# Moving the eight block transposes of each attention visit from the attention-times-values loop of the visit before into the scores loop of the visit itself

## The chip, the cores and the metric

The kernel runs on the 8 cores of one Trainium2 chip. Every core runs the same program on its own rows of the sequence. The metric is the device time in microseconds of the slowest core. Traces show one core: here core 7, the slowest of the profiled execution.

## What is computed

The reference is one transformer layer over a sequence of 16384 rows of 4096 numbers: a layer norm, an attention with four heads of width 1024 whose queries, keys and values are the normed input times a sign vector, a sigmoid in place of a softmax, a causal mask, a residual, and then a layer norm and a feed-forward step with a low-rank addition.

```python
xh = layernorm(x).reshape(B, T, 4, 1024)
Q, K, V = xh * q_bind, xh * k_bind, xh * v_bind
scores = einsum('bthd,bshd->bhts', Q, K) * 1024 ** -0.5
attn   = where(causal, sigmoid(scores * 4.0), 0.0)
x = x + einsum('bhts,bshd->bthd', attn, V)
x = x + ffn(layernorm(x))        # x @ W.T + bias, and a rank-16 term
```

## The kernel before

**Tiles.** The sequence is cut into 16 blocks of 1024 rows. Core c owns the query blocks c and 15 - c (q = 0 and 1). The attention goes through 8 *sweeps*, one for each query block and head (q outer, h inner). A sweep with q = 0 goes over 8 key blocks k, one with q = 1 over 16, so there are 4 x 8 + 4 x 16 = 96 *visits* (q, h, k). I number them 0 to 95. Sweeps begin at visits 0, 8, 16, 24, 32, 48, 64 and 80. After the attention comes the feed-forward part, which the change doesn't touch.

**One visit** is made by these pieces of the program, which write instructions into one list for each engine. Every engine runs its own list in order.

- `plan_visit_prep` (line 473): eight 512 KB loads on SyncE's queue bring the raw key block, one subtile of 128 rows each, into two buffers `khd`. VectorE normalises each subtile into `xb` (line 488). A load into a `khd` buffer waits until VectorE has normalised what was in it, so only two loads can run ahead of VectorE. Then one 1 MB load of the mask `msk` is issued, which waits until the masks of the visit before were used. It returns eight *tasks*; each task is `plan_xpose` (line 372) for one subtile: eight 128x128 transposes on TensorE into a PSUM buffer `ptr` (line 383, two buffers) and one copy by VectorE into `xbT` (line 394).
- `plan_qk_sig` (line 505): for each of eight key subtiles `sc`, TensorE waits for the copy into `xbT` of that subtile, and makes two groups of eight matmuls (line 517) into one of four PSUM banks. ScalarE takes the sigmoid of each group (line 531), VectorE multiplies it by the mask into `attn` (line 539). If statistics tasks are left, one follows each group: a 1 MB load on GpSimd's queue into one of two buffers `kh`, a VectorE sum (line 331) and two ScalarE sums of squares (lines 335, 338). Every 17th task is a short chain of small VectorE operations and a square root (lines 350 to 371). There are 272 tasks; they fill the first 16 visits and nine groups of visit 16.
- `plan_av` (line 552): 16 groups of eight matmuls (line 563) into two PSUM banks `pav`; VectorE adds each group into `acc` (line 580).
- `plan_epilogue` (line 594), after the last visit of a sweep: two small matmuls (line 597), their copies (line 602), and for each of eight subtiles two VectorE operations (lines 615, 617) and a store from one buffer `ebuf`.
- `plan_qg_prep`, ahead of each sweep: eight loads, each followed by a VectorE normalisation (line 417), eight transposes (line 430) and eight VectorE multiplies (line 441).

**The order before** is written out by the loop at line 671. For visit i the lists get: scores of visit i; then, if i + 1 starts a sweep, `plan_qg_prep`; then the eight normalisations of visit i + 1; then attention-times-values of visit i, in which after every second group one transpose task of visit i + 1 follows; then the epilogue, if visit i ends a sweep. So on VectorE the eight normalisations of the next visit stand ahead of the sixteen adds into `acc` of this one.

Of the kernel before, what the change touches and what calls it, by code (L numbers as in the profile page):

```python
# [25 lines left out]
def build_program():  # L26
# [24 lines left out]
    def ap_(e, fn):  # L51
        plan[e].append(fn)

    def W(e, sem, v):
        if v <= 0 or hiw[e][sem] >= v:
            return
        hiw[e][sem] = v
        ap_(e, lambda E, s=sem, vv=v: E.wait_ge(SEM[s], vv))
# [7 lines left out]
    def op(e, sem, build, n=1):  # L66
        if e in SERIAL:
            W(e, SERIAL[e], cnt[SERIAL[e]])
        v = bump(sem, n)
        ap_(e, lambda E, b=build, s=sem, k=n: b(E).then_inc(SEM[s], k))  # L70
        return v

    def opq(e, build):
        if e in SERIAL:
            op(e, SERIAL[e], build)
            return
        ap_(e, lambda E, b=build: b(E))
# [20 lines left out]
    with contextlib.ExitStack() as SH:  # L98
# [176 lines left out]
        with contextlib.ExitStack() as AT:  # L275
# [226 lines left out]
                         for st in range(NS)]  # L502
                return evs, mdv, tasks

            def plan_qk_sig(q, h, k, evs, mdv):
                b = k % 2
                gi = 0
                ttv = 0
                for sc in range(NS):
                    W("t", "V", evs[sc])  # L510
                    for th in range(2):
                        bank = gi % 4
                        qk_bank[bank].acquire("t")
                        qv = None
                        for dc in range(NS):
                            bf_ = (lambda E, dc=dc, sc=sc, th=th, b=b, bank=bank:
                                   E.matmul(  # L517
                                       pqk[bank][:],
                                       xbT[b][:, HD * dc + 128 * sc:HD * dc + 128 * (sc + 1)],
                                       QgT[:, CH * dc + 512 * th:CH * dc + 512 * (th + 1)],  # L520
                                       start=(dc == 0), stop=(dc == NS - 1)))
                            if dc == NS - 1:
                                qv = op("t", "T", bf_)
                            else:
                                opq("t", bf_)
                        state["qk_last"] = qv
                        ss = gi % 2
                        stage_slot[ss].acquire("s")
                        W("s", "T", qv)
                        W("s", "G", g_const)  # L530
                        sgv = op("s", "S", lambda E, ss=ss, bank=bank: E.activation(  # L531
                            out=stage[ss][:], in_=pqk[bank][:], func=AF.Sigmoid,
                            scale=cst[:, 0:1]))
                        qk_bank[bank].release([("S", sgv)])
                        W("v", "S", sgv)
                        W("v", *mdv)
                        W("v", "T", state["attn_war"])
                        ttv = op("v", "V", lambda E, ss=ss, sc=sc, th=th:
                                 E.tensor_tensor(  # L539
                                     attn[:, CH * sc + 512 * th:CH * sc + 512 * (th + 1)],  # L540
                                     stage[ss][:],
                                     msk[:, CH * sc + 512 * th:CH * sc + 512 * (th + 1)],
                                     OP.mult))
                        stage_slot[ss].release([("V", ttv)])
                        gi += 1
                        if stat_tasks:
                            stat_tasks.popleft()()
                            stat_drained[0] += 1
                msk_slot.release([("V", ttv)])
                return ttv  # L550

            def plan_av(q, h, k, ttv, xtasks):
                b = k % 2
                W("t", "V", ttv)
                gj = 0
                for tc in range(NS):
                    for dh in range(2):
                        bank = gj % 2
                        av_bank[bank].acquire("t")
                        avv = None  # L560
                        for sc in range(NS):
                            bf_ = (lambda E, sc=sc, tc=tc, dh=dh, b=b, bank=bank:
                                   E.matmul(  # L563
                                       pav[bank][:],
                                       attn[:, CH * sc + 128 * tc:CH * sc + 128 * (tc + 1)],
                                       xb[b][:, HD * sc + 512 * dh:HD * sc + 512 * (dh + 1)],
                                       start=(sc == 0), stop=(sc == NS - 1)))
                            if sc == NS - 1:
                                avv = op("t", "T", bf_)
                            else:  # L570
                                opq("t", bf_)
                        state["av_last"] = avv
                        W("v", "T", avv)
                        dst = acc[:, CH * tc + 512 * dh:CH * tc + 512 * (dh + 1)]
                        if k == 0:
                            sv = op("v", "V", lambda E, d=dst, bank=bank:
                                    E.tensor_copy(d, pav[bank][:]))
                        else:
                            sv = op("v", "V", lambda E, d=dst, bank=bank:
                                    E.scalar_tensor_tensor(  # L580
                                        out=d, in0=pav[bank][:], scalar=1.0, in1=d,
                                        op0=OP.mult, op1=OP.add))
                        av_bank[bank].release([("V", sv)])
                        gj += 1
                        if gj % 2 == 0 and xtasks:
                            xtasks.pop(0)()
                while xtasks:
                    xtasks.pop(0)()
                xb_slot[b].release([("T", state["av_last"])])
                xbT_slot[b].release([("T", state["qk_last"])])  # L590
                state["attn_war"] = state["av_last"]
# [69 lines left out]
            def drain_stats_until(kind, idx):  # L661
                tgt = stat_group_end.get((kind, idx), 0)
                while stat_drained[0] < tgt and stat_tasks:
                    stat_tasks.popleft()()
                    stat_drained[0] += 1

            plan_qg_prep(0, sweeps[0][0], sweeps[0][1])
            evs0, mdv0, tasks0 = plan_visit_prep(sweeps[0][0], sweeps[0][1], 0)
            for t_ in tasks0:
                t_()  # L670
            prepped = {0: (evs0, mdv0)}

            for fi, (sidx, q, h, k, L) in enumerate(flat):
                evs, mdv = prepped.pop(fi)
                ttv = plan_qk_sig(q, h, k, evs, mdv)
                ntasks = []
                if fi + 1 < len(flat):
                    nsidx, nq, nh, nk, nL = flat[fi + 1]
                    if nk == 0:
                        if nh == 0:  # L680
                            drain_stats_until("q", nq)
                        plan_qg_prep(nsidx, nq, nh)
                    if nh == 0:
                        drain_stats_until("kv", nk)
                    nevs, nmdv, ntasks = plan_visit_prep(nq, nh, nk)
                    prepped[fi + 1] = (nevs, nmdv)
                plan_av(q, h, k, ttv, ntasks)
                if k == L - 1:
                    plan_epilogue(sidx, q, h)

            fin = dict(cnt)

# [271 lines left out]
```

How the kernel before makes its waits and increments, by code:

```python
    def W(e, sem, v):  # L54
        if v <= 0 or hiw[e][sem] >= v:
            return
        hiw[e][sem] = v
        ap_(e, lambda E, s=sem, vv=v: E.wait_ge(SEM[s], vv))
# [7 lines left out]
    def op(e, sem, build, n=1):  # L66
        if e in SERIAL:
            W(e, SERIAL[e], cnt[SERIAL[e]])
        v = bump(sem, n)
        ap_(e, lambda E, b=build, s=sem, k=n: b(E).then_inc(SEM[s], k))
        return v
```

## Time and profile before

| | us |
|---|---|
| median of 3 runs | 12455.98 |
| the 3 runs | 12455.98, 12600.02, 12022.85 |
| profiled execution, whole | 11592.07 |
| profiled execution, span of core 7 | 11590.5 |
| spans of the 8 cores in it | 11547.0 to 11590.5 |

The profiled execution is shorter than each of the three runs. All sums in this document are made against it, since all durations come from it.

On the page, times are in microseconds unless marked ns. PE is TensorE's matmuls, PEld its weight loads, DVE is VectorE, ACT ScalarE, POOL GpSimd, SP SyncE. L563 is line 563 of the kernel before. In a timeline each row is: start, duration, engine, line, operation, output<-inputs, shapes, count, and in brackets the idle time just before and what ended it. Rows with the same operation in a run are merged. In a table of windows the columns are: the window, its length, the busy time and the number of instructions of PE, PEld, DVE, ACT and POOL, TensorE's granted clock as a share of the full one, the busy share of the DMA engines, and GB/s.

### The profile page before, as it was taken

How to read it: one execution, taken by the hardware profiler on the slowest of the kernel's cores; microseconds unless marked ns; L12 is line 12 of the kernel's file. 1: busy time of each engine (PE TensorE's matmuls, PEld its weight loads, DVE VectorE, ACT ScalarE, POOL GpSimd, SP SyncE). 2: the span in 40 equal slices, each digit the busy share in tenths (PEclk: the TensorE clock that was granted, in tenths of full speed). 3: DMA queues.
4: the chain of work that ended last, by engine and by line, in shares of the span. 5: the costliest groups of instructions: out<-in, count | busy, mean ns of one | idle time of the engine just before them, and what ended most of it. 6: DMA issues, size and time to landing. Idle time of an engine off the chain costs nothing.

```text
span 11590.5 us, 107337 instructions; the slowest of 8 cores (11547.0 to 11590.5 us)
## 1 busy us (share of the span) xinstructions
PE 7240.2 (62%) x36337; PEld 3343.7 (29%) x36337; DVE 4714.1 (41%) x6433; ACT 1864.7 (16%) x2891; POOL 260.1 (2%) x494
## 2 busy tenths in 40 slices
PE   0055545554775766777567775777757777378488
PEld 0022212221332332333233332333323333123233
DVE  2455555554444444444444444444444444410300
ACT  0234423331111111111011110111101111100100
POOL 0000000000000000000000000000000000000000
PEclk9987767777887888888888887888878888689699
DMA  9555544454222222121322122212131212144233
GB/s 110 153 170 175 174 132 166 167 174 129 75 69 73 73 69 77 55 73 55 80 66 73 55 73 73 73 55 73 55 91 55 73 55 73 44 105 98 67 80 91
DMA packets 503829, 1065.63 MB, mean 92 GB/s; under 512 B 315829, under 2 KB 315845, under 8 KB 451013
## 3 DMA queue, kind: packets, MB, share of 16 engines
q1 hardware_dynamic: 445336, 672.85, 20.1%
q0 software_dynamic: 57952, 385.92, 11.2%
q8 instruction: 298, 4.88, 0.2%
q14 instruction: 243, 1.99, 0.1%
HBM read 974.72 MB, written 83.89 MB: 91 GB/s over the span
## 4 chain that ended last, share of the span: by engine, by line
PE 53%; DMA 24%; DVE 11%; issue 5%; ACT 3%; SPq 2%; another core or an unknown queue 1%; DVEq 1%; ACTq 0%; POOLq 0%; POOL 0%
PE pav L563 22%; PE pqk L517 19%; DMA khd<-xk 14%; PE py L863 8%; DMA kh<-xk 5%; DVE xb L488 3%; PE ptr L383 3%; SPq L84 2%; DMA x1s<-ebuf 2%; DVE QgT L441 1%; ACT sdump L335 1%; ACT stage L531 1%; DVE suc L331 1%; DMA kh<-xq 1%
## 5 line engine op out<-in xcount | busy, mean ns | idle before, releaser
L563 PE MATMUL pav<-xb,attn 128*128 128x512 bf16 x12288 | 3016.3, 402 | 2189.0 <-DVE acc L580 1675.5
L517 PE MATMUL pqk<-QgT,xbT 128*128 128x512 bf16 x12288 | 2828.4, 392 | 699.8 <-ACT stage L531 687.7
L563 PEld LDWEIGHTS pav<-xb,attn 128*128 128x128 bf16 x12288 | 1222.4, 102 | 3700.7 <-issue 2567.7
L531 ACT ACTIVATE stage<-pqk,cst 128x512 bf16<-128x512 f32 x1536 | 1055.7, 687 | 6703.2 <-PE pqk L517 5825.9
L517 PEld LDWEIGHTS pqk<-QgT,xbT 128*128 128x128 bf16 x12288 | 1215.3, 100 | 2270.8 <-issue 944.6
L539 DVE TENSOR_TENSOR attn<-stage,msk 128x512 bf16<-128x512 bf16 x1536 | 1063.6, 692 | 1527.9 <-ACT stage L531 1523.4
L580 DVE SCALAR_TENSOR_TENSOR acc<-pav,acc 128x512 f32<-128x512 f32 x1408 | 974.1, 692 | 1262.8 <-PE pav L563 1217.5
L488 DVE TENSOR_SCALAR xb<-khd,mcache,rcache 128x1024 bf16<-128x1024 f32 x768 | 624.0, 813 | 1491.1 <-DMA khd<-xk 1469.7
L863 PE MATMUL py<-wtb,h2T 128*128 128x512 bf16 x4096 | 917.1, 382 | 221.0 <-DMA wtb<-wb 221.0
L331 DVE TENSOR_REDUCE suc<-kh 128x1 f32<-128x2048 f32 x288 | 658.3, 2286 | 264.6 <-DMA kh<-xk 196.7
L863 PEld LDWEIGHTS py<-wtb,h2T 128*128 128x128 bf16 x4096 | 392.9, 98 | 737.3 <-issue 290.6
L394 DVE COPY xbT<-ptr 128x1024 bf16<-128x1024 bf16 x768 | 531.4, 692 | 81.7 <-DVE acc L580 1.8
L884 DVE SCALAR_TENSOR_TENSOR yb<-py,xsl 128x512 f32<-128x512 f32 x128 | 88.6, 692 | 1109.4 <-PE py L873 1109.4
L383 PE MATMUL ptr<-ident,xb 128*128 128x128 bf16 x6144 | 471.7, 220 | 46.2 <-DVE xb L488 28.1
L383 PEld LDWEIGHTS ptr<-ident,xb 128*128 128x128 bf16 x6144 | 409.4, 98 | 229.0 <-issue 52.3
L335 ACT ACTIVATE sdump<-kh 128x1024 bf16<-128x1024 f32 x288 | 304.3, 1056 | 719.0 <-DMA kh<-xk 375.6
L430 PE MATMUL ptr<-ident,qtm 128*128 128x128 bf16 x512 | 63.5, 302 | 451.6 <-DVE qtm L417 451.6
L338 ACT ACTIVATE sdump<-kh 128x1024 bf16<-128x1024 f32 x288 | 304.3, 1056 | 26.9 <-ACT sdump L335 0.7
L787 PE MATMUL ptrF<-ident,fb 128*128 128x128 bf16 x512 | 64.8, 306 | 373.0 <-DVE fb L776 373.0
L746 ACT ACTIVATE sdump<-fb 128x1024 bf16<-128x1024 bf16 x64 | 67.6, 1056 | 889.1 <-DMA fb<-x1s 884.7
L615 DVE TENSOR_TENSOR ebuf<-acc,vbsl 128x1024 bf16<-128x1024 f32 x64 | 78.4, 1225 | 301.7 <-DMA x1s<-ebuf 300.9
L441 DVE TENSOR_SCALAR QgT<-ptr,gT 128x128 bf16<-128x128 bf16 x512 | 145.4, 284 | 135.1 <-PE ptr L430 85.4
(110 smaller groups left out, 1292.5 us busy)
## 6 DMA issues: line engine op xcount, KB each, us to landing
khd<-xk SPq DMA_DIRECT2D x768, 512.0 KB, 5.0
kh<-xk POOLq DMA_DIRECT2D x256, 1024.0 KB, 5.5
msk<-mk SPq DMA_DIRECT2D x96, 1024.0 KB, 8.6
khd<-xq SPq DMA_DIRECT2D x128, 512.0 KB, 4.3
wb<-wgt POOLq DMA_DIRECT2D x4, 8192.0 KB, 202.0
kh<-xq POOLq DMA_DIRECT2D x32, 1024.0 KB, 6.1
y<-yb POOLq DMA_DIRECT2D x128, 256.0 KB, 2.3
x1s<-ebuf POOLq DMA_DIRECT2D x64, 256.0 KB, 4.5
```

The source lines that it names most:

```text
L331: opq("v", lambda E, col=col: E.reduce_sum(suc[:, col:col + 1], kr_ap, axis=AX))
L335: opq("s", lambda E, col=col: E.activation(out=sdump[:], in_=kr_ap[:, 0:1024], func=AF.Square, accum_out=sqa[:, 2 * col:2 * col + 1]))
L338: sv = op("s", "S", lambda E, col=col: E.activation(out=sdump[:], in_=kr_ap[:, 1024:2048], func=AF.Square, accum_out=sqa[:, 2 * col + 1:2 ...
L383: bf_ = (lambda E, dc=dc, xo=xb_buf, c0=st * HD, p=ps: E.transpose(ptr[p][:, 128 * dc:128 * (dc + 1)], xo[:, c0 + 128 * dc:c0 + 128 * (dc ...
L394: ev = op("v", "V", lambda E, d=dst, s_=src: E.tensor_copy(d, s_))
L488: E.tensor_scalar(out=xb[b][:, st * HD:(st + 1) * HD], in0=khd[ks][:], scalar1=mcache[:, 8 * k + st:8 * k + st + 1], scalar2=rcache[:, 8 * ...
L517: E.matmul(pqk[bank][:], xbT[b][:, HD * dc + 128 * sc:HD * dc + 128 * (sc + 1)], QgT[:, CH * dc + 512 * th:CH * dc + 512 * (th + 1)], star ...
L531: sgv = op("s", "S", lambda E, ss=ss, bank=bank: E.activation(out=stage[ss][:], in_=pqk[bank][:], func=AF.Sigmoid, scale=cst[:, 0:1]))
L539: E.tensor_tensor(attn[:, CH * sc + 512 * th:CH * sc + 512 * (th + 1)], stage[ss][:], msk[:, CH * sc + 512 * th:CH * sc + 512 * (th + 1)], ...
L563: E.matmul(pav[bank][:], attn[:, CH * sc + 128 * tc:CH * sc + 128 * (tc + 1)], xb[b][:, HD * sc + 512 * dh:HD * sc + 512 * (dh + 1)], star ...
L580: E.scalar_tensor_tensor(out=d, in0=pav[bank][:], scalar=1.0, in1=d, op0=OP.mult, op1=OP.add))
L863: E.matmul(py[bank][:], h2T[:, 1024 * dc + 128 * tc:1024 * dc + 128 * (tc + 1)], wtt[:, 512 * dc:512 * (dc + 1)], start=(dc == 0), stop=Fa ...
```

## The change

It reorders the program's lists; no operation is added or taken away. The transpose tasks of a visit go from `plan_av` of the visit before to `plan_qk_sig` of the visit itself: one ahead of each subtile `sc`. And all preparation of visit i + 1 (query preparation, rest of the statistics, loads and normalisations) now follows `plan_av` and the epilogue of visit i, where it stood ahead of them.

```diff
-            def plan_qk_sig(q, h, k, evs, mdv):
+            def plan_qk_sig(q, h, k, evs, mdv, xtasks):
...
                 for sc in range(NS):
+                    if xtasks:
+                        xtasks.pop(0)()
                     W("t", "V", evs[sc])
...
-            def plan_av(q, h, k, ttv, xtasks):
+            def plan_av(q, h, k, ttv):
...
-                        if gj % 2 == 0 and xtasks:
-                            xtasks.pop(0)()
-                while xtasks:
-                    xtasks.pop(0)()
...
-            prepped = {0: (evs0, mdv0)}
+            prepped = {0: (evs0, mdv0, [])}
...
-                evs, mdv = prepped.pop(fi)
-                ttv = plan_qk_sig(q, h, k, evs, mdv)
-                ntasks = []
+                evs, mdv, xtasks = prepped.pop(fi)
+                ttv = plan_qk_sig(q, h, k, evs, mdv, xtasks)
+                plan_av(q, h, k, ttv)
+                if k == L - 1:
+                    plan_epilogue(sidx, q, h)
                 if fi + 1 < len(flat):
...
                     nevs, nmdv, ntasks = plan_visit_prep(nq, nh, nk)
-                    prepped[fi + 1] = (nevs, nmdv)
-                plan_av(q, h, k, ttv, ntasks)
-                if k == L - 1:
-                    plan_epilogue(sidx, q, h)
+                    prepped[fi + 1] = (nevs, nmdv, ntasks)
```

## Rows read from the trace of the kernel before

**Rows 1.** The page: busy time by engine, share of the span, instructions.

```profile
PE 7240.2 (62%) x36337; PEld 3343.7 (29%) x36337; DVE 4714.1 (41%) x6433; ACT 1864.7 (16%) x2891; POOL 260.1 (2%) x494
```

**Rows 2.** The waits: engine, tile and line, waiting for; us in total, times, longest.

```profile
PE pav L563 <- DVE acc L580: 1675.5, 87, 25.0
```

**Rows 3.** Timeline of an ordinary visit inside a sweep, TensorE and VectorE.

```profile
6063.02 27.79 PE L517 MATMUL pqk<-QgT,xbT 128*128 128x512 bf16 x128
...
6092.62 1.74 DVE L488 TENSOR_SCALAR xb<-khd,mcache,rcache 128x1024 bf16<-128x1024 f32 x2
...
6092.66 3.61 PE L563 MATMUL pav<-xb,attn 128*128 128x512 bf16 x16 [1.85 <-DVE attn L539]
...
6113.34 0.81 DVE L488 TENSOR_SCALAR xb<-khd,mcache,rcache 128x1024 bf16<-128x1024 f32 x1 [3.98 <-DMA khd<-xk]
...
6115.09 5.96 PE L563 MATMUL pav<-xb,attn 128*128 128x512 bf16 x16 [18.37 <-DVE acc L580]
...
6120.89 0.61 PE L383 MATMUL ptr<-ident,xb 128*128 128x128 bf16 x8
...
6121.34 3.62 PE L563 MATMUL pav<-xb,attn 128*128 128x512 bf16 x16
...
6122.03 0.69 DVE L394 COPY xbT<-ptr 128x1024 bf16<-128x1024 bf16 x1
```

**Rows 4.** Windows that hold whole visits, from scores start to scores start.

```profile
734.50:1520.40 785.90, 431.82 (x1925) 181.55 (x1923) 438.35 (x463) 303.24 (x498) 50.67 (x96) 0.77 0.50 169
1520.40:1878.40 358.00, 157.47 (x710) 67.69 (x708) 187.18 (x231) 97.30 (x160) 20.69 (x39) 0.69 0.47 150
1878.40:2650.10 771.70, 431.79 (x1924) 183.12 (x1922) 424.62 (x457) 289.43 (x474) 47.94 (x90) 0.77 0.48 164
2650.10:2987.70 337.60, 149.72 (x709) 66.69 (x707) 171.13 (x236) 80.38 (x130) 15.42 (x29) 0.72 0.40 128
3506.60:3684.50 177.90, 72.07 (x386) 35.76 (x386) 79.83 (x138) 10.99 (x16) 4.34 (x8) 0.68 0.31 89
8711.50:9858.30 1146.80, 856.55 (x4483) 406.65 (x4481) 478.54 (x673) 153.99 (x224) 0.00 (x0) 0.88 0.21 65
```

**Rows 5.** Timeline of visit 95, which has no next visit to prepare.

```profile
9887.96 27.79 PE L563 MATMUL pav<-xb,attn 128*128 128x512 bf16 x128 [1.85 <-DVE attn L539]
...
9915.92 0.69 DVE L580 SCALAR_TENSOR_TENSOR acc<-pav,acc 128x512 f32<-128x512 f32 x1 [1.03 <-PE pav L563]
```

**Rows 6.** Timeline of a sweep's end (visits 23, 24), TensorE and VectorE.

```profile
3508.39 0.81 DVE L417 TENSOR_SCALAR qtm<-khd,omc,orc 128x1024 bf16<-128x1024 f32 x1
...
3551.11 0.81 DVE L488 TENSOR_SCALAR xb<-khd,mcache,rcache 128x1024 bf16<-128x1024 f32 x1
...
3572.57 0.81 DVE L488 TENSOR_SCALAR xb<-khd,mcache,rcache 128x1024 bf16<-128x1024 f32 x1 [4.07 <-DMA khd<-xk]
...
3603.00 0.60 PE L597 MATMUL pqk<-vbrow,ones_b 1*128 1x512 bf16 x2
...
3662.13 1.23 DVE L617 TENSOR_TENSOR ebuf<-ebuf,khd 128x1024 bf16<-128x1024 bf16 x1
```

**Rows 7.** Timeline of visit 6's end, with statistics tasks.

```profile
1441.21 2.29 DVE L331 TENSOR_REDUCE suc<-kh 128x1 f32<-128x2048 f32 x1
...
1460.17 5.54 PE L563 MATMUL pav<-xb,attn 128*128 128x512 bf16 x16 [16.31 <-DVE attn L539]
...
1462.52 0.17 DVE L350 TENSOR_TENSOR ve<-suc 128x8 f32<-128x8 f32 x1
...
1467.95 0.17 DVE L371 TENSOR_TENSOR rcache<-r,t 128x8 f32<-128x8 f32 x1
```

**Rows 8.** Timeline of visit 7's scores: TensorE after rests of different length.

```profile
1537.37 3.57 PE L517 MATMUL pqk<-QgT,xbT 128*128 128x512 bf16 x8 [4.42 <-ACT stage L531]
...
1546.87 6.55 PE L517 MATMUL pqk<-QgT,xbT 128*128 128x512 bf16 x16 [3.01 <-ACT stage L531]
```

**Rows 9.** The mask's load, from issue to landing.

```profile
DMA to landing us min/median/max: 6.6/8.6/9.9
```

## The prediction

> **What bounds the kernel now.** I read the busy shares first. TensorE is the busiest engine with 62% of the span, VectorE has 41% [rows 1]: no engine is full, so the order of work and its waits set the time. The list of waits names the one to look at: the attention-times-values matmuls wait 1675.5 us in 87 places for the adds into `acc` [rows 2]. Then I read the timeline of an ordinary visit, one without statistics tasks and inside a sweep [rows 3]. The scores take 27.79 us without a break, 0.217 us a matmul, so TensorE is at its full clock of 2.4 GHz there. It rests 1.85 us until the last sigmoid and mask multiply are through. It makes two groups of attention-times-values (3.61 us) and stops for 18.37 us: both PSUM banks are full, and VectorE, which must empty them, has the eight normalisations of the next visit ahead of them in its list. These run from 6092.62 to 6113.34 + 0.81 = 6114.15, a stretch of 21.5 us in which VectorE mostly waits for loads, since two buffers let only two loads run ahead. After the stop the first 16 matmuls take 5.96 us where the next 16 take 3.62: 2.3 us for the clock. Then 8 transposes (0.61 us on TensorE) follow every second group, and their copy by VectorE (0.69 us) runs beside the matmuls and holds up nobody. Fourteen such visits take 1146.8 us [rows 4], 81.9 us each.
>
> **Part 1: the stop in attention-times-values goes.** After the change VectorE's list has the 16 adds right behind the mask multiplies. Visit 95 shows what that gives, as it has nothing to prepare: 128 matmuls in 27.79 us [rows 5]. In an ordinary visit before, the same matmuls with the transposes took 81.9 - 27.8 - 1.85 = 52.3 us.
>
> **Part 2: the same stop comes back ahead of the scores.** The normalisations now start after the last add. The scores need the first copy into `xbT`, and that stands behind all eight normalisations on VectorE. From the end of the matmuls: last add through 0.86 us later (9915.92 + 0.69, against 9887.96 + 27.79 [rows 5]), 0.1 to the next instruction, the stretch of normalisations, 0.1 + 0.69 for the copy [rows 3], 0.06 to TensorE. The stretch is 21.5 us in one visit [rows 3] and 22.3 in another [rows 6]; I take 22.0. Nothing in it is sped up: the buffers are still two, and the first two loads were ready before too. So TensorE rests 0.86 + 0.1 + 22.0 + 0.85 = 23.8 us, where it rested about 19. Before, two groups of matmuls lay beside the stretch; now nothing does but the first transposes, 0.61 us. The slow start of the clock, 2.2 us, moves with the stop.
>
> **Part 3: a lockstep inside the scores.** This decides the case. The copy for subtile sc + 1 now stands on VectorE behind both mask multiplies of subtile sc, and TensorE waits for that copy before the next matmul. Its four banks no longer let it run ahead. The row that prices the wait is the 1.85 us between scores and attention-times-values [rows 3]: it is the same chain, last matmul, sigmoid, mask multiply, next matmul. The copy adds 0.69 + 0.06. So each of seven places costs 1.85 + 0.75 = 2.60 us; the transposes fit inside it, since TensorE does them while ScalarE works. That is 18.2 us a visit. Lower bound: the chain can't be shorter than its three durations, about 2.1 us, or 14.7 a visit.
>
> **The ordinary visit after:** scores 27.8 + 2.2 + 18.2 = 48.2; 1.85; attention-times-values 27.8; rest 23.8. Sum 101.6, against 81.9: **+19.7 us**. In parts: the stop +4.5, lockstep +18.2, the transposes leave the other loop -3.1. There are 73 such visits (17 to 94 without the five that end a sweep): +1,440 us.
>
> **The clock in the lockstep.** After the 1.85 us rest the next matmuls run at the full rate, 3.61 us for 16, each time [rows 3]. After rests of 4.42 and 3.01 us they ran at about half rate (3.57 us for 8, 6.55 for 16) [rows 8]. In the lockstep TensorE does 0.61 us of transposes and then rests 2.0 us, so I keep the full rate; the other case is a rival below. The Trainium skill (TensorE: Matmul & The Clock Gate, section "HAM oscillation — how this bites in real kernels") says that short bursts of matmuls between waits can each start at the half clock; by that rule each pair of groups in the lockstep would be slow if the rest were long enough. The rests of 3.01 and 4.42 us agree with it, the one of 1.85 us lies on the other side.
>
> **Sweep ends.** Before, the epilogue on VectorE ran beside only four groups of the next scores, and the query preparation beside nothing. Now everything is in one row. From scores end to scores end: 1.85 + 27.8 + epilogue 60.4 (3603.0 to 3662.13 + 1.23) + query preparation 42.7 (3508.39 to 3551.11) + normalisations 22.3 (to 3572.57 + 0.81) [rows 6] + 0.85 + 48.2 = 204.1, against 177.9 [rows 4]: +26.2, five times: +131.
>
> **Visits with statistics.** Each group there brings a 2.29 us sum on VectorE and 2.5 us on ScalarE. Before, the loads set the pace and TensorE waited 16.31 us at the end of the scores [rows 7]. After, I follow one subtile from the copy: first group at half clock 3.4 (3.57 in [rows 8]), sigmoid 0.9, multiply 0.85, sum 2.4; second multiply 0.7 and sum 2.4, copy 0.75, and some 0.4 in which the second sigmoid waits for the slow second group: 11.8 us. With the clock up it would be 10.0. The scores with their tail are 7 x 11.8 + 8.65 = 91.2. Visits 1 to 6 then take 91.2 + 27.8 + 23.8 + 5.6 for the last statistics task (1462.52 to 1467.95 + 0.17 and a gap [rows 7]), which had stood elsewhere: 148.5 against 785.9 / 6 = 131.0, +105 for six. Visits 9 to 14: 142.8 against 771.7 / 6 = 128.6, +85. Visits 7 and 8: 91.2 + 27.8 + 60.4 + 42.7 + 22.3 + 0.85 = 245.3, and 142.8, against 358.0: +30. Visits 15 and 16 (nine tasks in 16): 245.3 + 125.2 against 337.6: +33 [rows 4]. Visit 0 has no lockstep: -4. Visit 95: +20. Together +269.
>
> **Costs at nothing.** SyncE's queue: the order of loads is the same but for the sweep ends, where the epilogue's loads now precede the preparation's; they have the same two buffers and are paced by VectorE either way. The mask load is issued about 8 us before the normalisations end and takes at most 9.9 us [rows 9]; its first reader now comes some 5 us after their end, so about 3 us are to spare. If that cover went, each microsecond of lateness would be 95 us in all. GpSimd's queue: the stores of the epilogue wait for VectorE as before; behind them stand only statistics loads.
>
> **The sum:** 1,440 + 131 + 269 = +1,840 us. 11,592 + 1,840 = **13,430 us** for an execution like the profiled one. The three runs of before lie 431 to 1,008 us above that execution, and no row says why. The matmuls are the same after, so some of it will be there too; TensorE rests more, so I take the smallest: 13,430 + 430 = **13,860 us**.
>
> The Trainium skill (TensorE: Matmul & The Clock Gate, section "Seeing it yourself") says that dense matmuls on three or more cores of a die are held below the full clock; the profiled execution shows nothing of it, with 0.217 us a matmul.
>
> **The rivals.**
> - *The clock falls in the lockstep.* For it: the rests of 3 us and more [rows 8]. Against: 1.85 us never did. 16 matmuls would take 6.55 instead of 3.47 us: +3.1 in seven places of 79 visits, +1,700. 15,130 us on the profiled basis.
> - *The stretch of normalisations shrinks*, because the loads land faster once attention-times-values no longer runs beside them. Against: only 3.6 us of matmuls ran beside them before, and these don't load anything. Its floor is 8 x 0.81 = 6.5 us, 15.4 less in 79 visits, -1,220: 12,210 us, still slower than 11,592 by 5%.
> - *Not slower: what lengthens the runs outside the profile is spared.* If the 431 to 1,008 us come from dense matmul stretches, and the looser stretches after escape them altogether, after stands at 13,430 and before at up to 12,600. That is +6.6%. To end within 2%, before would have to gain 1,590 us that after does not; the highest run shows 1,008. The place is the 27.8 us stretches of scores, which the lockstep breaks up.
>
> **How the numbers follow.** The forecast has 0.86, the clock 0.08, the shorter stretch 0.04, the spared excess 0.02. The range reaches down to 13,430 less the warm statistics chain (1.8 x 8 x 15 = 216), so 13,200, and up to 13,430 + 1,008 and some 150 for the terms, 14,600. It leaves out the clock rival and the shorter stretch, 0.12 together. About 2% is what a measurement of this kernel can tell from no change; even the floor of the stretch lies outside it. Slower by over 2%: 0.97; within: 0.02; faster: 0.01.
>
> **What the profile after would show.** The wait of the `pav` matmuls for `acc` gone, and their 128 in 27.8 us. In the scores, 16 matmuls, 8 transposes, and then a rest of about 2.0 us ended by the copy into `xbT`, seven times a visit; a first rest of about 23 us. Visits of 101.6 us. VectorE's busy time unchanged at 4,714 us. If the rest in the scores is near 1 us, or the pairs take 6.5 us, part 3 is wrong; if the first rest is far from 23, part 2; if visits with statistics are not longer by 14 to 17 us, their chain.

## The result and the profile after

| | us |
|---|---|
| changed kernel, median of 9 runs | 14428.37 (13901.96 to 14566.09) |
| kernel before, median of 10 runs | 12082.18 (11587.66 to 12639.78) |
| ratio of comparable runs | 1.205, 95% interval 1.190 to 1.220 |
| least disturbed execution, before and after | 11,588 and 13,902: +2,314 |

The forecast was slower, 13,860 us in a range of 13,200 to 14,600; the kernel is slower, at 14,428. Every one of its nine runs is longer than the longest of the kernel before. The runs of one kernel spread here by 2 to 13%, because in some of them the cores of one die or both show a lower granted clock, so what follows compares the runs and cores without it, called undisturbed. The cores of the profiled execution of the changed kernel:

```profile
core 0: 13921.1 us, clock 0.815
core 1: 13908.7 us, clock 0.816
...
core 5: 14332.1 us, clock 0.787
```

I read core 0, whose span is within 0.2% of the 13,902 us. It stands against the 13,430 us of the forecast for an execution like the profiled one of before: the sum was 490 us short, 1,840 where some 2,330 came. Its waits answer to [rows 2]:

```profile
PE pqk L519 <- DVE xbT L394: 3931.1, 760, 23.0
DVE attn L541 <- ACT stage L533: 3718.0, 1518, 6.2
```

The matmuls into `pav`, which waited 1675.5 us for `acc` before [rows 2], wait for it nowhere now. In place of that wait the scores' matmuls wait 3931.1 us for the copy into `xbT`, in 760 places: eight for each of visits 1 to 95. Busy time didn't move: VectorE has 4713.6 us on the page of the changed kernel, 4714.1 before [rows 1]. All the loss is waiting and clock: VectorE makes nothing more than before, but TensorE waits for it in more places.

The timeline of core 0, from the end of one visit through the scores of the next (line 565 is attention-times-values, 519 the scores, 541 the mask multiply, 383 and 394 the transposes and their copy):

```profile
7012.32 0.69 DVE L541 TENSOR_TENSOR attn<-stage,msk 128x512 bf16<-128x512 bf16 x1 [1.05 <-ACT stage L533]
7013.16 27.79 PE L565 MATMUL pav<-xb,attn 128*128 128x512 bf16 x128 [1.85 <-DVE attn L541]
...
7041.92 1.73 DVE L488 TENSOR_SCALAR xb<-khd,mcache,rcache 128x1024 bf16<-128x1024 f32 x2
...
7062.31 0.81 DVE L488 TENSOR_SCALAR xb<-khd,mcache,rcache 128x1024 bf16<-128x1024 f32 x1 [2.23 <-DMA khd<-xk]
7063.23 0.69 DVE L394 COPY xbT<-ptr 128x1024 bf16<-128x1024 bf16 x1
7064.17 5.24 PE L519 MATMUL pqk<-QgT,xbT 128*128 128x512 bf16 x16 [20.68 <-DVE xbT L394]
...
7072.17 3.61 PE L519 MATMUL pqk<-QgT,xbT 128*128 128x512 bf16 x16 [2.31 <-DVE xbT L394]
7074.21 0.69 ACT L533 ACTIVATE stage<-pqk,cst 128x512 bf16<-128x512 f32 x1 [3.95 <-PE pqk L519]
7075.07 0.69 DVE L541 TENSOR_TENSOR attn<-stage,msk 128x512 bf16<-128x512 bf16 x1 [3.15 <-ACT stage L533]
7075.62 0.61 PE L383 MATMUL ptr<-ident,xb 128*128 128x128 bf16 x8
7075.94 0.69 ACT L533 ACTIVATE stage<-pqk,cst 128x512 bf16<-128x512 f32 x1 [1.04 <-PE pqk L519]
7076.79 0.69 DVE L541 TENSOR_TENSOR attn<-stage,msk 128x512 bf16<-128x512 bf16 x1 [1.03 <-ACT stage L533]
7077.59 0.69 DVE L394 COPY xbT<-ptr 128x1024 bf16<-128x1024 bf16 x1
7078.54 3.61 PE L519 MATMUL pqk<-QgT,xbT 128*128 128x512 bf16 x16 [2.31 <-DVE xbT L394]
...
7091.27 5.30 PE L519 MATMUL pqk<-QgT,xbT 128*128 128x512 bf16 x16 [2.31 <-DVE xbT L394]
...
7099.32 3.61 PE L519 MATMUL pqk<-QgT,xbT 128*128 128x512 bf16 x16 [2.31 <-DVE xbT L394]
```

Attention-times-values runs through in 27.79 us, as in [rows 5]. It starts 0.15 us after the end of the last mask multiply (7012.32 + 0.69). The normalisations take 21.2 us (7041.92 to 7062.31 + 0.81), as before, now with TensorE at rest. Then comes the lockstep, to be followed from 7072.17: matmuls, sigmoid at 7075.94, mask multiply at 7076.79, copy at 7077.59, next matmuls at 7078.54. And one pair of groups, at 7091.27, takes 5.30 us instead of 3.61.

The last 14 whole visits of this core, from scores start to scores start (columns as in [rows 4]):

```profile
10674.50:12164.20 1489.70, 913.97 (x4481) 416.19 (x4482) 478.61 (x672) 153.89 (x224) 0.00 (x0) 0.86 0.16 50
```

That is 106.4 us a visit; [rows 4] has 81.9 and the forecast 101.6.

### The profile page after: what moved, and what is told of

Its sections match the earlier page's. It is cut to its first block, busy times and chain, and to the rows that moved or that the text cites. A ratio compares the mean times of both kernels' runs of the same rounds, so it can differ in the third digit from the quotient of the medians.

```text
span 14332.1 us, 107914 instructions; the slowest of 8 cores (13908.7 to 14332.1 us)
## 1 busy us (share of the span) xinstructions
PE 8099.5 (57%) x36337; PEld 3545.8 (25%) x36337; DVE 4713.6 (33%) x6433; ACT 1864.7 (13%) x2891; POOL 259.6 (2%) x494
## 4 chain that ended last, share of the span: by engine, by line
PE 53%; DVE 17%; DMA 15%; issue 6%; ACT 6%; SPq 2%; another core or an unknown queue 1%; DVEq 1%; ACTq 0%; POOLq 0%; POOL 0%
PE pqk L519 24%; PE pav L565 20%; DMA khd<-xk 11%; PE py L860 7%; ACT stage L533 4%; DVE attn L541 4%; DVE xbT L394 4%; DVE xb L488 3%; DVE suc L331 2%; SPq L84 2%; DMA x1s<-ebuf 2%; DVE QgT L441 1%; DVEq L58 1%; ACT sdump L335 1%
## 5 line engine op out<-in xcount | busy, mean ns | idle before, releaser
L519 PE MATMUL pqk<-QgT,xbT 128*128 128x512 bf16 x12288 | 3572.8, 456 | 3966.0 <-DVE xbT L394 3947.4
L565 PE MATMUL pav<-xb,attn 128*128 128x512 bf16 x12288 | 2816.1, 394 | 207.9 <-DVE attn L541 207.9
L519 PEld LDWEIGHTS pqk<-QgT,xbT 128*128 128x128 bf16 x12288 | 1335.4, 113 | 5950.1 <-issue 5257.9
L860 PE MATMUL py<-wtb,h2T 128*128 128x512 bf16 x4096 | 1080.8, 431 | 221.4 <-DMA wtb<-wb 221.4
L860 PEld LDWEIGHTS py<-wtb,h2T 128*128 128x128 bf16 x4096 | 428.7, 107 | 865.1 <-issue 800.9
L430 PEld LDWEIGHTS ptr<-ident,qtm 128*128 128x128 bf16 x512 | 49.5, 138 | 852.7 <-issue 852.7
L84 POOL DMA_DIRECT2D x1s<-ebuf x64 | 34.6, 541 | 9486.2 <-DVE ebuf L615 9486.2
```

The costliest lines, as they stand in the source:

```text
L84: E.dma_start(out=o, in_=i, **kww), 16)
L519: E.matmul(pqk[bank][:], xbT[b][:, HD * dc + 128 * sc:HD * dc + 128 * (sc + 1)], QgT[:, CH * dc + 512 * th:CH * dc + 512 * (th + 1)], star ...
L565: E.matmul(pav[bank][:], attn[:, CH * sc + 128 * tc:CH * sc + 128 * (tc + 1)], xb[b][:, HD * sc + 512 * dh:HD * sc + 512 * (dh + 1)], star ...
L860: E.matmul(py[bank][:], h2T[:, 1024 * dc + 128 * tc:1024 * dc + 128 * (tc + 1)], wtt[:, 512 * dc:512 * (dc + 1)], start=(dc == 0), stop=Fa ...
```

## Experiments

Theory L: the lockstep in the scores is the bulk of the loss. Rival P: the normalisations, now exposed, are. Theory K: what is missing in the sum is TensorE's clock, which falls in the short rests of the lockstep. Two kernels part L from P by undoing one half of the change each; two change the length of the rest, one in each direction; the changed kernel itself runs beside them once more; and one takes the stop out of the kernel before without making a lockstep.

### One half undone: transposes a subtile ahead

```diff
                 for sc in range(NS):
-                    if xtasks:
+                    while xtasks and len(xtasks) > NS - 2 - sc:
                         xtasks.pop(0)()
```

> Changed kernel, but each transpose task is written one subtile earlier: tasks 0 and 1 ahead of the first scores, task sc + 1 ahead of the scores of subtile sc, so the copy into xbT stands on VectorE ahead of the mask multiplies and TensorE needn't wait for them. The preparation stays behind attention-times-values. Theory L (the lockstep is the bulk of the loss): the seven rests in the scores go, 7 x 2.9 us and about 3.0 us of slow clock, and 7 x 0.43 us of transposes come into the open: an ordinary visit of 106.4 becomes 86 us, with the rest of 23.5 us ahead of the scores kept. In all some 1,800 us less than the changed kernel: 12,100 us, 4 to 5% over before. Rival P (the exposed normalisations are the bulk): the visit stays above 100 us and the kernel near 13,900 us.

Measured: 11,903 us undisturbed (11,924 in a second run, 12,307 and 12,901 in the other two) against 11,593 of before beside it. The wait and the timeline of core 2 of this kernel:

```profile
PE pqk L519 <- DVE xbT L394: 2049.7, 144, 21.8
...
7016.73 1.49 DVE L394 COPY xbT<-ptr 128x1024 bf16<-128x1024 bf16 x2
7017.67 5.90 PE L519 MATMUL pqk<-QgT,xbT 128*128 128x512 bf16 x16 [19.33 <-DVE xbT L394]
7023.41 0.61 PE L383 MATMUL ptr<-ident,xb 128*128 128x128 bf16 x8
7023.86 3.62 PE L519 MATMUL pqk<-QgT,xbT 128*128 128x512 bf16 x16
7025.38 0.69 DVE L394 COPY xbT<-ptr 128x1024 bf16<-128x1024 bf16 x1
7027.31 0.61 PE L383 MATMUL ptr<-ident,xb 128*128 128x128 bf16 x8
7027.76 3.62 PE L519 MATMUL pqk<-QgT,xbT 128*128 128x512 bf16 x16
```

and its last 14 whole visits:

```profile
8929.40:10126.50 1197.10, 863.51 (x4480) 406.81 (x4480) 478.52 (x673) 153.89 (x224) 0.00 (x0) 0.86 0.18 62
```

85.5 us a visit, where L wanted 86 and P over 100. The wait for the copy stands in 144 places instead of 760. There is no rest at all between the pairs, and the only slow pair is the first one, behind the long rest. 2,000 of the 2,314 us are gone with one line, 200 more than L said. What stays, 310 us, goes with the new place of the preparation: the rest ahead of the scores is there as in the changed kernel. P falls.

### The other half undone: preparation back in its old place

```diff
                 ttv = plan_qk_sig(q, h, k, evs, mdv, xtasks)
-                plan_av(q, h, k, ttv)
-                if k == L - 1:
-                    plan_epilogue(sidx, q, h)
                 if fi + 1 < len(flat):
...
                     prepped[fi + 1] = (nevs, nmdv, ntasks)
+                plan_av(q, h, k, ttv)
+                if k == L - 1:
+                    plan_epilogue(sidx, q, h)
```

> The other half: preparation of the next visit back ahead of attention-times-values, as in the kernel before, but the transposes one subtile at a time inside the scores, as in the changed kernel. Theory L: an ordinary visit is 81.9 - 3.1 for the transposes + 1.9 for the first copy + 7 x 2.9 + 3.0 for the clock = 104 us, the kernel 13,650 us, 17 to 18% over before. Rival P: about as before, 82 us a visit and 11,600 us.

Measured: 13,850 us undisturbed, the lowest of six runs (up to 14,654), where P wanted 11,600 and L 13,650. The waits of core 4 in the profiled execution, whose span is 14,181 us:

```profile
PE pqk L519 <- DVE xbT L394: 2485.8, 760, 62.3
PE pav L565 <- DVE acc L582: 1675.2, 87, 26.4
```

Both waits are there side by side: the old stop, 1675.2 us where [rows 2] has 1675.5, and a wait for the copy in the same 760 places as in the changed kernel. The lockstep alone costs about as much as the whole change. The two halves cost 310 and 2,260 us, more together than the 2,314 of the whole. Two terms of the expectations are in the halves and not in the whole: the transposes that lie in the open in the first half (7 x 0.43 us a visit), and the 1.9 us for the first copy in this one. That they make up the difference is an argument; no run takes it apart.

### The rest filled with transposes nobody needs

```diff
+                for dc in [d for _r in range(2) for d in range(NS)]:
+                    opq("t", lambda E, dc=dc, xo=xb_buf, c0=st * HD, p=ps:
+                        E.transpose(
+                            ptr[p][:, 128 * dc:128 * (dc + 1)],
+                            xo[:, c0 + 128 * dc:c0 + 128 * (dc + 1)], ident[:]))
                 for dc in range(NS):
```

> Changed kernel with each group of eight transposes in a visit done three times into the same PSUM buffer (the same result, 16 more transposes of 0.056 us each a subtile, about 0.9 us). They lie in the rest of 2.3 us before the copy, whose start the sigmoids and mask multiplies set, so by themselves they cost nothing. Theory K (in a quarter of the subtiles the clock has fallen in the rest, which makes 16 matmuls 5.2 us instead of 3.6): with a rest of 1.4 us no pair starts slow, the visit goes from 106.4 to 103.4 us and the kernel from 13,900 to about 13,650 us, though it does more. If the slow pairs come from something else, they stay, and the time is 13,900 or more.

Measured: 14,033 to 14,620 us in four runs, which alone would not tell it from the changed kernel. But in the shortest of them cores 4 to 7 took 13,635 to 13,681 us, where the same four cores took 13,839 to 13,894 in a run of the changed kernel. That speaks for K, and the profile of a second measurement settles it.

> The kernel with the filled rest once more, beside the changed kernel on the same chip, for a profile that can be compared pair by pair. Theory K: no pair of groups behind a rest of 1.4 us takes 5.0 us or more where the changed kernel has about one in four at 5.2; the visit is 103.4 us and the span 13,650 us. Otherwise the slow pairs stay.

Measured: 13,687 and 13,695 us in two of four runs (14,386 and 14,449 in the others). The timeline of TensorE on core 5 (line 524 is the scores, 384 the added transposes, 388 the needed ones):

```profile
7071.65 3.61 PE L524 MATMUL pqk<-QgT,xbT 128*128 128x512 bf16 x16 [1.41 <-DVE xbT L399]
7075.10 1.06 PE L384 MATMUL ptr<-ident,xb 128*128 128x128 bf16 x16
7076.00 0.61 PE L388 MATMUL ptr<-ident,xb 128*128 128x128 bf16 x8
7078.02 3.61 PE L524 MATMUL pqk<-QgT,xbT 128*128 128x512 bf16 x16 [1.41 <-DVE xbT L399]
...
10482.20:11933.50 1451.30, 976.75 (x6272) 507.78 (x6273) 478.51 (x672) 153.93 (x224) 0.00 (x0) 0.89 0.16 51
```

The pair still starts 6.37 us after the one before (7071.65 to 7078.02), as in the changed kernel (7072.17 to 7078.54): the added work lies wholly in the rest. But of 540 such pairs that the trace shows as one row after the statistics visits, all 540 take 3.61 us; on core 0 of the changed kernel 389 of 526 do, and 137 take 5.0 to 5.3. The visit is 103.7 us instead of 106.4, and the kernel 215 us faster with 12,288 more transposes. K holds. The added work does two things at once, though: it shortens the rest and gives TensorE more to do between two pairs. Which of the two keeps the clock up, this run can't tell.

### The rest made longer: each copy twice

```diff
+                opq("v", lambda E, d=dst, s_=src: E.tensor_copy(d, s_))
                 ev = op("v", "V", lambda E, d=dst, s_=src: E.tensor_copy(d, s_))
```

> Changed kernel with each copy into xbT made twice (the same result). VectorE's busy time grows by 96 x 8 x 0.69 = 530 us. Theory L: the copy is on the path of every subtile, so each of the eight places costs 0.8 us more, 6.4 us a visit, 610 us in all, and the wait of the scores' matmuls for the copy grows by as much. Theory K adds: the rest of TensorE grows from 2.3 to 3.1 us, so more pairs of groups start with the clock down, up to all seven a visit where about one in four does now: up to 8.5 us a visit more. So 14,500 us with L alone, up to 15,300 with K at its most, against 13,900 of the changed kernel. If the copy lay beside other work, nothing would be added.

Measured: 15,378 us, the lowest of four runs (up to 15,729). Rows of core 7 (span 15,243), its wait for the copy, pairs of scores and the window of the last 14 visits:

```profile
PE pqk L520 <- DVE xbT L395: 4551.2, 760, 24.8
...
7005.32 3.61 PE L520 MATMUL pqk<-QgT,xbT 128*128 128x512 bf16 x16 [3.10 <-DVE xbT L395]
...
7029.82 5.30 PE L520 MATMUL pqk<-QgT,xbT 128*128 128x512 bf16 x16 [3.10 <-DVE xbT L395]
...
7038.68 6.49 PE L520 MATMUL pqk<-QgT,xbT 128*128 128x512 bf16 x16 [3.10 <-DVE xbT L395]
...
11763.70:13473.60 1709.90, 1043.97 (x4480) 448.93 (x4481) 556.06 (x784) 154.42 (x224) 0.00 (x0) 0.78 0.14 43
```

The rest grew from 2.31 to 3.10 us, by the 0.79 of a copy and its gap: the copy lies on the path, as L says. The wait for it grew from 3931.1 to 4551.2 us, by 620 where L said 610. Of the 553 pairs behind a short rest in visits 17 to 95 only 104 are at full speed now, 309 take 4.8 to 5.4 us and 140 take 6.3 to 6.6. The starts of the single matmuls in the trace say what these times are: 0.216 us apart at full clock, 0.427 at half. A pair of 6.5 us has 13 or 14 of its 15 intervals at half clock, one of 5.3 us has 8. And not all slow pairs start slow: the one at 7029.82 has four intervals at full clock and only then eight near half. Of the 553 pairs 273 start at half clock and 176 fall to it after three to six intervals. The last 14 visits take 122.1 us each, 15.7 more than in the changed kernel: 6.4 for the copies, some 9 for the clock, where K at its most had said 8.5. Over all 73 ordinary visits it is 121.2 against 106.5, some 8 for the clock.

### The changed kernel beside them

> The changed kernel itself, beside the two others on the same chip, as their measure. Span 13,900 us; TensorE's rests before the copy 2.3 us, about one pair of groups in four at 5.2 us instead of 3.6.

Measured: 14,390 to 14,910 us in six runs. In the profiled one cores 0 to 3 took 13,865 to 13,900 us, where the eight cores of the kernel with the filled rest took 13,639 to 13,693 beside it. Core 1 shows 400 of 534 pairs at 3.6 us and 134 at 5.0 to 5.3: the share of slow pairs is a quarter again.

### A version that beats both: normalisations between the groups

It starts from the kernel before. Each normalisation is a task too, and `plan_av` takes one ahead of every two groups; the mask load follows the last.

```diff
-            def plan_av(q, h, k, ttv, xtasks):
+            def plan_av(q, h, k, ttv, xtasks, ntask):
...
                 for tc in range(NS):
+                    if ntask:
+                        ntask.pop(0)()
                     for dh in range(2):
```

> Kernel before, but the eight normalisations of the next visit are not ahead of attention-times-values: one stands ahead of each two groups of it, the transposes of that subtile after them as before, the mask load after the last. VectorE then has two adds, a normalisation and a copy (2.9 us) to each 3.9 us of TensorE, and the loads get 3.9 us each where they took 2.75. If the stop in attention-times-values comes only from the order on VectorE's list, it goes and doesn't come back: a visit of 27.8 + 1.85 + 27.8 + 8 x 0.43 = 61 us against 81.9, some 1,900 us less than before, 9,700 us. If the loads can't keep that pace beside the matmuls, a rest of a few us stays ahead of every second pair and the visit is 65 to 75 us.

Measured: 9,571 us undisturbed, 10,073 the median of six runs, against 11,593 and 11,940 of before beside it: 17% less undisturbed (the expectation said 9,700 us), and 31% less than the changed kernel's 13,902. Core 5 (line 573 is attention-times-values, 489 the normalisation, 590 the add):

```profile
6049.29 3.62 PE L573 MATMUL pav<-xb,attn 128*128 128x512 bf16 x16
6049.98 0.69 DVE L394 COPY xbT<-ptr 128x1024 bf16<-128x1024 bf16 x1
6050.78 0.81 DVE L489 TENSOR_SCALAR xb<-khd,mcache,rcache 128x1024 bf16<-128x1024 f32 x1
6051.69 0.69 DVE L590 SCALAR_TENSOR_TENSOR acc<-pav,acc 128x512 f32<-128x512 f32 x1
6052.75 0.61 PE L383 MATMUL ptr<-ident,xb 128*128 128x128 bf16 x8
6053.09 0.69 DVE L590 SCALAR_TENSOR_TENSOR acc<-pav,acc 128x512 f32<-128x512 f32 x1 [0.70 <-PE pav L573]
6053.19 3.62 PE L573 MATMUL pav<-xb,attn 128*128 128x512 bf16 x16
...
6959.20:7812.90 853.70, 827.44 (x4483) 400.03 (x4481) 478.15 (x673) 154.18 (x224) 0.00 (x0) 1.00 0.28 87
```

In each 3.90 us of TensorE VectorE does a copy, a normalisation and two adds and still waits 0.70 us for TensorE; no wait for a load is listed for these 14 visits. The visit is 61.0 us, to the tenth what was expected, with a granted clock of 1.00 over the window: the stop took the slow restart with it.

## Why the prediction was right, and where its sum was short

**Slower, by a lockstep: right.** Both halves of the change, each alone, show that part 3 of the prediction is the bulk of the loss: without the lockstep 310 of 2,314 us are left, with the lockstep alone 2,260 come. The stop in attention-times-values goes (part 1) and comes back ahead of the scores (part 2): the time from the end of its matmuls to the scores is 23.5 us on average, forecast 23.8. The stretch of normalisations stayed at 21 to 22 us; the rival by which it shrinks didn't happen. VectorE's busy time didn't change. The mask load was nowhere waited for.

**The price of one place in the lockstep: 2.90 us, not 2.60.** A pair starts 6.37 us after the last where the sum had 3.47 + 2.60. Two small errors add up. The 1.85 us were a rest counted from the modelled end of the last matmul, which lies 3.61 us behind the start of a pair, and I added them to the 3.47 us that a pair takes inside an unbroken run: 0.14 us lost. And I gave the copy 0.69 + 0.06: it starts 0.11 us behind the mask multiply, and TensorE starts 0.26 us behind its end (7077.59 + 0.69 to 7078.54), where it starts 0.15 behind a mask multiply (7013.16). The copy adds 0.11 + 0.69 + 0.26 - 0.15 = 0.91. Seven places make 2.1 us a visit. The term "lockstep +18.2" measured 20.3.

**"So I keep the full rate": the step that failed.** I took the 1.85 us rest, never followed by slow matmuls, as the nearest row to a rest of 2.0, and put the whole clock into a rival in which all pairs would be slow, by 3.1 us each. The 1.85 us rest was no bad reading: in the changed kernel too it is never followed by slow matmuls (0 of 77 visits on core 0). But the rest in the lockstep is 2.3 us, and 137 of 526 pairs are slow by about 1.65 us: 0.26 x 7 x 1.65 = 3.0 us a visit. The forecast was one case, its rival the other, and the chip did a quarter of the rival's pairs at about half of its price for each. The run with the filled rest and the one with the longer rest show that it hangs on what happens between the pairs: none, a quarter, four fifths of the pairs have a slow stretch where the rests are 1.4, 2.3 and 3.1 us. Why a quarter, and not all or none, no run shows.

**The sum, then,** on core 0. Ordinary visits 106.47 on average instead of 101.6: 73 x 4.9 = +355 (2.1 + 3.0 - 0.3 for the rest ahead of the scores). Sweep ends 208.6 instead of 204.1, +23. Visits 0 to 16 together about +105: the chain there took 93.6 us from scores start to attention-times-values in the first sweep (forecast 91.2), and 96.5 in the second, for which I have no experiment. Visits 1 to 6 and 9 to 14 became 22 us longer on average, more than the 14 to 17 that the prediction had set as the sign that their chain was right. The three terms add up to some 485 of the 490.

**From the profiled basis to the median.** I had added 430 us, the least that the three runs of before showed. The median of the changed kernel lies 526 us above its least disturbed run (14,428 - 13,902). In the kernel before it lies 494 us above. With all the 490 us that the sum lacked the forecast would have been 14,350. That the looser stretches are spared what lengthens the runs is not borne out. Some luck is in the range: its top allowed 150 us for errors of the sum, and they came to 490. The median lies inside it because the top also held 1,008 us for what lengthens the runs, of which the median took 526.

**The rival on the other side** asked for an excess of 1,590 us in the kernel before alone. Its runs now reach from 11,588 to 12,640, those of the changed kernel from 13,902 to 14,566: both have it, the changed kernel somewhat less in these runs (664 us against 1,052) but as much in a later measurement (up to 14,910).

## What to carry to other kernels

Before moving work to another loop, write down for each engine what stands in its list ahead of the thing that the next step waits for: a copy of 0.69 us cost 2.9 us a time, not because it was long but because it stood behind two other engines' answers, and one subtile of lead took the whole price away. A stop caused by a block of work on a neighbour engine is not cured by moving the block as a whole; dealt out one piece to every two groups of matmuls it fitted into the neighbour's idle time, and the kernel became 17% faster than before. Price a rest of TensorE by what it does to the next matmuls, read from rows with rests of its own length, and as a share of cases: neither the all nor the none of the prediction came.

## What the runs showed of the hardware

In these kernels TensorE's clock didn't turn from full to half at one length of rest. With bursts of 3.5 us of matmuls and 0.6 us of transposes, a rest of 2.3 us let a quarter of the bursts start at 1.2 GHz and left the others at 2.4 (137 of 526 on core 0, 134 of 534 on core 1 of another execution). The slow ones came singly: on these two cores no slow pair follows a slow pair directly in the scores of a visit. With rests of 1.4 us all of 540 pairs ran at 2.4 GHz. With rests of 3.1 us four fifths had a stretch at 1.2 GHz; about half of all started slow, and a third started at full clock and fell within the burst. The runs change the rest and the share of time in which TensorE works together, so they don't say which of the two counts.

The mean granted clock over whole visits doesn't show this by itself. It was 0.89, 0.86 and 0.78 in the kernels with rests of 1.4, 2.3 and 3.1 us, but also 0.88 in the kernel before [rows 4] and 0.86 in the one with the transposes a subtile ahead, which have no such rests: each of these five has a stop of some 20 us a visit. It was 1.00 where neither the stop nor the short rests were there. The duration of the single bursts tells them apart.

Transposes that nobody needs paid in a rest that is there anyway: 12,288 of them made the kernel 215 us faster.

The rule that the prediction weighed (the Trainium skill, TensorE: Matmul & The Clock Gate, section "HAM oscillation — how this bites in real kernels") describes bursts that start at half clock after each wait. The trace agrees for a part of them: with rests of 2.3 us it was a quarter.
